# One constants load, x laid out by partition, and the input normalisation split into three groups

## The reference, cut to what matters

```python
def _ln(x, w, b):
    mu = jnp.mean(x, axis=-1, keepdims=True)
    var = jnp.mean(jnp.square(x - mu), axis=-1, keepdims=True)
    return (x - mu) * jax.lax.rsqrt(var + EPS) * w + b
...
ln_out = _ln(hidden_states, ln_w, ln_b)
q = _fp8_linear_pertensor(ln_out, wq, wq_scale, q_in_scale).reshape(b, s, g, hpg, d)
q = _ln(q, qln_w, qln_b)
...
x = x + jnp.tanh(g_xattn[0]) * _L0_xattn_ref(_layernorm(x, axis=-1), ctx_2048, ...)
x = x + jnp.tanh(g_ffn[0]) * _L0_ffn_ref(_layernorm(x, axis=-1), ...)
```

## Time and profile before

| | |
|---|---|
| median of 3 runs | 439.84 us |
| the three runs | 439.84, 442.92, 439.6 us |
| the profiled execution | 438.61 us |
| its span, from first to last instruction | 436.8 us |
| busy of the span: PE, DVE, ACT, POOL | 89%, 81%, 67%, 64% |
| first projection starts | 19.53 us |

### The profile page before, as it was taken

One profiled execution on the slowest core, in us unless ns is written; L12 is line 12 of the kernel. 1 busy time (PEld: TensorE's weight loads), 2 busy tenths in 40 slices (PEclk: granted clock), 3 DMA queues, 4 the chain that ended last, 5 costly groups with the idle time before them and its releaser, 6 DMA issues.

```text
span 436.8 us, 11224 instructions
## 1 busy us (share of the span) xinstructions
PE 387.8 (89%) x3626; PEld 288.6 (66%) x3626; DVE 352.9 (81%) x804; ACT 294.6 (67%) x621; POOL 278.0 (64%) x379
## 2 busy tenths in 40 slices
PE   0577799999999999999999999999998497999970
PEld 0445567667667767676766777676687286999960
DVE  5867979999999998999999999999889762334336
ACT  2598788777877777876877787787973315666510
POOL 2068866886787687688588677765574750366650
PEclk9999999999999999999999999999989688999995
DMA  8960868999980000000000000000194213444308
GB/s 209 261 228 2 106 90 259 253 287 286 243 230 3 0 0 0 0 0 0 0 0 0 0 0 0 0 2 2 33 434 194 96 67 98 124 132 136 99 22 277
DMA packets 34621, 45.57 MB, mean 104 GB/s; under 512 B 2970, under 2 KB 32031, under 8 KB 33696
## 3 DMA queue, kind: packets, MB, share of 16 engines
q1 hardware_dynamic: 26368, 35.34, 27.4%
q0 software_dynamic: 6944, 9.46, 9.9%
q10 hardware_dynamic: 1280, 0.41, 0.5%
HBM read 28.21 MB, written 24.19 MB: 120 GB/s over the span
## 4 chain that ended last, share of the span: by engine, by line
PE 73%; DVE 11%; ACT 4%; DMA 4%; issue 3%; POOL 3%; POOLq 0%; ACTq 0%; SPq 0%; DVEq 0%
PE proj_ps L972 18%; PE proj_ps L964 8%; PE score_ps L1001 8%; PE pv_ps L1024 8%; PE headT_ps L990 6%; PE out_ps L1034 6%; PE proj_ps L1138 4%; PE headT_ps L1138 3%; PE score_ps L990 3%; PE probT_ps L1010 3%; DMA cenf<-in_cen 2%; PE score_ps L1153 1%; DVE xs L1702 1%; DVE arena L1326 1%; PE pv_ps L1153 1%
## 5 line engine op out<-in xcount | busy, mean ns | idle before, releaser
L972 PE MATMUL proj_ps<-arena 128*128 128x512 f16 x384 | 100.0, 383 | 3.0 <-DVE arena L1356 3.0
L1364 DVE BATCH_NORM_STATS2 st<-rot 128x6 f32<-128x256 f32 x192 | 72.6, 419 | 10.6 <-ACT rot L710 10.0
L572 POOL TENSOR_TENSOR rot<-rot,cw 128x512 f32<-128x512 f32 x64 | 77.9, 1238 | 2.5
L710 ACT ACTIVATE rot<-proj_ps 128x512 f32<-128x512 f32 x96 | 56.1, 585 | 7.6 <-PE proj_ps L972 6.0
L972 PEld LDWEIGHTS proj_ps<-arena 128*128 (+1 forms) x384 | 32.5, 98 | 32.3 <-issue 3.8
L642 POOL DMA_INDIRECT ybuf<-arena,bslot x31 | 30.5, 984 | 31.3 <-DVE bslot L1612 14.6
L731 ACT ACTIVATE rot<-rot,cw 128x128 f32<-128x128 f32 x128 | 40.9, 391 | 11.0 <-POOL cw L566 10.4
L578 POOL TENSOR_TENSOR reg<-reg,rinv 128x512 f32<-128x512 f32 x32 | 33.4, 1044 | 21.9 <-DVE rinv L1374 21.9
L964 PE MATMUL proj_ps<-arena 128*128 128x512 f16 x192 | 46.7, 379 | 0.6 <-POOL arena L528 0.6
L1024 PEld LDWEIGHTS pv_ps<-reg,vv 64*128 64x128 f32 x512 | 31.1, 187 | 12.9 <-issue 9.7
L990 PE MATMUL headT_ps<-idf,rot 128*128 128x128 f32 x256 | 38.5, 273 | 0.1
(11 more groups left out here) (229 smaller groups left out, 850.2 us busy)
## 6 DMA issues: line engine op xcount, KB each, us to landing
zbuf<-fill SPq DMA_DIRECT2D x1, 16576.5 KB, 65.5
arena<-in_wffn SPq DMA_DIRECT2D x4, 1536.0 KB, 13.4
arena<-zbuf SPq DMA_DIRECT2D x30, 128.5 KB, 2.2
wkv_stage<-in_wkvN SPq DMA_DIRECT2D x1, 2048.0 KB, 15.4
wp_sb<-in_wpT POOLq DMA_DIRECT2D x1, 2048.0 KB, 16.4
wp_sb<-ybuf SPq DMA_DIRECT2D x8, 256.0 KB, 4.5
xs<-in_x SPq DMA_DIRECT2D x2, 512.0 KB, 5.5
vv<-in_wqN POOLq DMA_DIRECT2D x1, 1024.0 KB, 12.5
```

The costliest lines, as they stand in the source:

```text
L572: gp.tensor_tensor(r, r, cw[:, 4 * i:4 * i + 4].unsqueeze(2).to_broadcast([P, 4, D]), ALU.mult)\
L710: act.activation(raw[c % 2][i], proj_ps[i % 2][:, :], ACT.Copy).then_inc(proj_evac, 1)
L972: mm = pe.matmul(ps, lhs, w[kind][:, ch, 512 * b:512 * b + 512], start=(k == 0), stop=(k == 3))
L1364: ins = ve.bn_stats(st[:, 4 * i + h:4 * i + h + 2, :].rearrange("p h s -> p (h s)"), raw[c % 2][i][:, h * D:(h + 2) * D].rearrange("p (h d ...
```

## The change

The constants `colv`, `idf` and `cenf` are one tensor (`consts`) with one load, and three of the routing tables another (`tables`); the names in the code are now slices of these. ACT loads the table for Tanh ahead of the wait for the constants. x is laid out by partition on the host, so that each partition's part of a load is one contiguous run; it comes in three loads, tile 0, tiles 1 to 3, tiles 4 to 7 (`XG`). Statistics, root, sharpening and normalisation are done for each group apart. Folds 0 to 3 stand on PE ahead of the first projection, the transposes of tiles 1 to 3 behind it (they were ahead of it), and tiles 4 to 7 are normalised, transposed and moved out in the midst of step 0 (`inputs_variance(2)`, `inputs_root(2)`, `inputs_scale(2)`, `input_transposes(1)`, `inputs_out(1)`). The small operations on the gates move from the start into step 0. `xn` lies in other banks of `rot`.

```diff
+XG = [(0, 1), (1, NT // 2), (NT // 2, NT)]
...
-            for half in range(2):
-                sp.dma_start(xs[:, half * NHT * H:(half + 1) * NHT * H].rearrange("p (t d) -> p t d", t=NHT),
-                             x[half * NHT * P:(half + 1) * NHT * P, :].rearrange("(t p) d -> p t d", p=P))\
-                  .then_inc(ld_x[half], 16)
+            for i, (t0, t1) in enumerate(XG):
+                sp.dma_start(xs[:, t0 * H:t1 * H], x[:, t0 * H:t1 * H]).then_inc(ld_x[i], 16)
...
-            act.dma_start(colv[:, :], cols).then_inc(ld_cols, 16)
-            act.dma_start(idf[:, :], ident).then_inc(ld_small, 16)
-            act.dma_start(cenf[:, :], cen).then_inc(ld_small, 16)
-            act.dma_start(rowv[:, :], rowc).then_inc(ld_route, 16)
-            act.dma_start(trif[:, :], tri).then_inc(ld_route, 16)
-            act.dma_start(slots[:, :], slot).then_inc(ld_route, 16)
+            act.dma_start(consts[:, :], cols).then_inc(ld_cols, 16)
+            act.preload_act_table(ACT.Tanh)
+            act.dma_start(tables[:, :], rowc).then_inc(ld_route, 16)
...
+            inputs_root(1)
+            for j in range(4):
+                fold_high(j)
...
                 if isinstance(n, int) and n == 0:
-                    inputs_out(1)
+                    inputs_out(0)
...
                 if proj:
                     evacuate(n, c, 1)
+                if isinstance(n, int) and n == 0:
+                    inputs_root(2)
...
                 if proj:
                     values_out(t, c)
+                if isinstance(n, int) and n == 0:
+                    inputs_out(1)
```

More of the change, by code:

```diff
@@ L71 @@
 NCOL = _n
+NCONST = NCOL + 2 * P
+NTABLE = NROWV + P + NT * TOPK
 BANKS = [("k", 0), ("q", 0), ("q", 1), ("v", 0),
@@ L161, in build @@
         xs = sb("xs", [P, NT * H], F32)
-        colv = sb("colv", [P, NCOL], F32)
-        rowv = sb("rowv", [P, NROWV], F32)
-        idf = sb("idf", [P, P], F32)
-        cenf = sb("cenf", [P, P], F32)
+        consts = sb("consts", [P, NCONST], F32)
+        colv, idf, cenf = consts[:, 0:NCOL], consts[:, NCOL:NCOL + P], consts[:, NCOL + P:NCONST]
+        tables = sb("tables", [P, NTABLE], F32)
+        rowv, trif = tables[:, 0:NROWV], tables[:, NROWV:NROWV + P]
+        slots = tables[:, NROWV + P:NTABLE].bitcast(U32)
         cenb = sb("cenb", [P, P], BF16)
@@ L329, in col @@
             return colv[:, a:a + 1]
-        ld_x = [sem("ld_x0"), sem("ld_x1")]
+        ld_x = [sem(f"ld_x{i}") for i in range(3)]
         ld_cols = sem("ld_cols")
-        ld_small = sem("ld_small")
         ld_ctx = sem("ld_ctx")
@@ L686, in fold_high @@
                 act.activation(dst, src, ACT.Copy, scale=scale).then_inc(fold_hi, 1)
-            for j in range(2):
-                fold_high(j)
             act.wait_ge(xT0_done, 1)
@@ L701, in inputs_out @@
                                    scale=col("lnw", c), bias=col("lnb", c)).then_inc(xT_evac, 1)
-            inputs_out(0)
-            for j in range(2, 4):
-                fold_high(j)
             def evacuate(n, c, i):
@@ L918, in fold @@
                 mm.then_inc(fold_done, 1)
-            pe.wait_ge(ld_small, 32)
-            pe.wait_ge(cen_done, 1)
-            for j in range(2):
-                fold(j)
+            pe.wait_ge(ld_cols, 16)
             pe.wait_ge(xn_done, 1)
@@ L939, in input_transposes @@
                     mm.then_inc(xT_done, 1)
-            input_transposes(0)
+            pe.wait_ge(cen_done, 1)
+            for j in range(4):
+                fold(j)
             def project(t, c, i):
@@ L1108, in step @@
                     project(t, c, 2)
+                if isinstance(n, int) and n == 0:
+                    input_transposes(1)
                 for j in next_folds(n, 2):
@@ L1118, in step @@
                     fold(j)
+                if isinstance(n, int) and n == 1:
+                    pe.wait_ge(xT_evac, 2 * HC)
                 if heads:
@@ L1122, in step @@
                     head_transposes(n - 1, before, 2)
-                if isinstance(n, int) and n == 0:
-                    pe.wait_ge(xT_evac, 2 * HC)
                 if isinstance(n, int) and n == NU - 1:
                     pe.wait_ge(ld_wp, 16)
-            for j in range(2, 4):
-                fold(j)
             def unit_up(u, z, w):
@@ L1268, in newton, with row_stats @@
                 link(ve.tensor_tensor(r, r, a, ALU.mult))
-            def row_stats(t0, t1, loads=None):
+            def row_stats(t0, t1, load):
+                ve.wait_ge(load, 16)
                 for t in range(t0, t1):
-                    if loads and t % NHT == 0:
-                        ve.wait_ge(loads[t // NHT], 16)
                     ins = ve.bn_stats(tst[:, t, :], xs[:, t * H:(t + 1) * H])
@@ L1326, in fold_low @@
                 ve.scalar_tensor_tensor(low, src, scale, high, ALU.mult, ALU.subtract).then_inc(fold_lo, 1)
-            for j in range(2):
-                fold_low(j)
             def inputs_clip(T):
@@ L1352, in _ @@
             inputs_mag(0)
+            for j in range(2):
+                fold_low(j)
             ve.wait_ge(xmag_done, 1)
@@ L1449, in step @@
                     fold_low(j)
+                if isinstance(n, int) and n == 0:
+                    inputs_variance(2)
                 if attend:
@@ L1459, in step @@
                     fold_low(j)
+                if isinstance(n, int) and n == 0:
+                    inputs_scale(2)
+                    rows_normal(*XG[2])
+                    output_gates()
                 if attend:
```

58 lines of the change are left out of this document (29 added, 29 removed).

## The result

| | before | with the change |
|---|---|---|
| median, lowest to highest, runs | 439.28 us, 437.86 to 447.04, 16 | 445.18 us, 443.13 to 446.64, 16 |
| ratio, with its 95% interval | | 1.0119 [1.0096, 1.0143] |
| the profiled execution, its span | 438.61, 436.8 us | 443.13, 441.3 us |
| first projection | 19.53 us | 16.45 us |
| root of step 0, of step 1 on ACT | 33.40, 47.05 us | 38.76, 52.43 us |

The ratio goes by the executions in the faster of two states alone and is therefore not the quotient of the medians, which are over all executions, slower ones of the kernel before (up to 447.96 us) and one of e4 at 2167.56 us included.

The account below looks back on a forecast made before the run. A chain of waits was taken to bound the start, the root of step 0 the rest: 4.0 us won, 7.9 lost in step 0, root 3.9 later; 438.61 becomes 442.5, plus 0.9 for a median gives 443.4 us (439.8 to 445.3).

Parts of the forecast that it names:

- likeliest case: Whole kernel: the root of step 0 comes 3.9 us later, the median is 443.4 us; chance 0.60.
- rival of late loads: Start: the joined load lands at 6.5 us or more, root 5.8 later, 445.3 us or more; chance 0.13.
- T, the landing of the joined constants: Start: the joined load of constants lands at 4.6 us, for the range up to 5.6.
- First projection: End of the start: it begins at T + 10.95, 15.55 us, which is 4.0 us earlier than before.
- The 0.4 that it takes off: Start, DVE's sum of 11.35 us: 0.4 off, as pieces added this way gave 9.15 for a stretch of 8.73.
- if the weights land no later: PE ahead of the first projection: folds 2 and 3 fit on this condition; a later landing costs one for one.
- The chain of tiles 4 to 7: Step 0: statistics, root, low of fold 10, sharpening (1.0 us) and tiles follow in one line, ending at 29.55 us.
- The pause and the clock: Middle of step 0: PE idles some 4.7 us, its clock falls to half, the last projection takes 1.86 us.
- rival that the clock stays up: Step 0 behind the pause: transposes, folds and projection take half, root at 35.3, 441.4 us; chance 0.17.
- From the tiles to the root: End of step 0: transposes, folds, last projection and ACT's copies bring the root from 29.55 to 37.3 us.
- Handed on in full: Behind step 0: POOL passes any shift of its root on in full, to the end of the kernel.
- Not slower, the work falls into idle time: Step 0: DVE's idle 4.3 us take all but 1.3 of 5.6 inserted, 2.7 gained, 436.8 us; chance 0.10.

Follow-up runs that it names:

- e4: The change with sharpening and normalising of tiles 4 to 7 behind the lows of folds 12 and 13, their transposes and evacuations ending step 0; 1.0018 of the kernel before.
- e7: The change with folds 2 and 3 behind the first projection on PE, so that it doesn't wait for the q weights; 1.0150 of the kernel before.
- e8: The change with one wait added: POOL's last cast of a fold waits until tiles 4 to 7 are normalised; 1.0099 of the kernel before.
- e5: The change with twenty unread matmuls on PE in the pause ahead of the transposes of tiles 4 to 7; 1.0083 of the kernel before.
- e11: e4 with the transposes behind step 1's first projection, evacuations behind its evacuation, gates behind step 0's first statistics; 437.84 us, 0.9964 of the kernel before.
- e3: The change with all work on tiles 4 to 7, statistics to evacuations, at the end of step 0 on every engine; 1.0268 of the kernel before.
- e9: The change with the work on tiles 4 to 7 spread over step 0, the tiles normalised behind the low of fold 8; 1.0014 of the kernel before.

## Why the prediction was right, and which term was too small

The direction, the mechanism and the range held: 443.4 (439.8 to 445.3) was predicted and 445.18 measured. By the prediction's own line of 1% the kernel is slower, just over it, and that had the chance 0.25; the likeliest case lay under the line since one term was too small. That the range holds is in part luck: 445.18 is 0.1 under its upper end, which was taken from the rival of late loads, and that rival fell.

- **T, the landing of the joined constants**: 4.6 predicted, 4.04 measured (3.92 to 4.80 in the runs that load them as one in the changed order). The rival of late loads fell.
- **First projection**: 15.55 predicted, 16.45 measured, 3.08 won and not 4.0. The sum on DVE was good (rounding ends 11.07 after the landing, where the prediction has 10.8). The 0.4 that it takes off was not needed: in e7, where no weights are waited for, the first projection starts 11.21 after the landing, and the pieces add up to 11.35; the 9.15 from which the 0.4 comes can't be had from the pieces listed, which give 9.09 without ACT's two copies and 9.52 with them. The step that failed is that folds 2 and 3 fit "if the weights land no later": they land 1.0 later. Of the 0.9 by which the projection is late, 0.4 is left at the end of the statistics of tiles 4 to 7; e7 takes the wait away and wins nothing, but by another order.
- **The chain of tiles 4 to 7**: statistics end 25.72 (25.35), root ends 26.20 (25.8), the low of fold 10 ends 27.56 (27.15), sharpening ends 29.67 (28.15), tiles end 31.09 (29.55). Up to the low of fold 10 all is 0.4 late, and every piece but one has the length that it was given. **The mis-sized term is the sharpening**: 1.0 was taken from the earlier trace rows, from a place where POOL does nothing; in step 0 POOL casts folds, and it took 2.2. Holding POOL back gives 1.03 at the root (e8), most of the 1.5 by which the root was predicted too early; the median is 1.3 lower, but the intervals of the two ratios overlap.
- **The pause and the clock**: 4.7 us of pause predicted, 5.81 measured; the last projection was to take 1.86 and took 1.92. The rival that the clock stays up was priced at a root 2.0 earlier (35.3 against 37.3); keeping PE busy gives 2.03 (e5). That rival fell, and its price was right. The lower level at the start is read from durations alone: the first projection takes 1.86 us before and 1.91 now, as long as at a granted clock of 0.50, while the column reads 1.00 there (19.5 to 21.5 and 16.4 to 18.4).
- **From the tiles to the root**: 7.75 predicted (29.55 to 37.3), 7.67 measured (31.09 to 38.76).
- **Handed on in full**: yes, 5.36 at the root and 5.35 to 5.38 at every root of the loop. ACT's wait for POOL in step 1 shrinks from 2.07 to 0.45 and still ends with POOL.
- **"Not slower, the work falls into idle time"**: it fell for this order, as PE and ACT have nothing to work on in the pause. e11 has the same work behind the first projection, in an order in which PE does have something to do, and ends 1.8 us before the kernel before, with up to 1.0 of it perhaps from the clock.

## What to carry to other kernels

Work that is pushed out of the start into the first step must be placed piece by piece: who waits for each piece, what stands behind it in that engine's order, and whether another engine has work for that time; here an early start that was followed by one pause of PE was paid back twice, by the pause and by the clock after it. The duration of a small DVE operation may be carried over only from a place where POOL does the same as in the new place. To know early what a reorder at the start will do to the end, compare one row behind it (here ACT's root of step 1); the medians of thirteen kernels followed it, with 0.06 to 2.62 us on top.

## What the runs showed of the hardware that I had not expected

- A DVE operation on 4 numbers per partition took 3.90 us beside a POOL instruction of 4.05, and 0.16 without one (e3, e8). Operations that read PSUM did not suffer: the lows of folds take 0.73 to 0.77 with POOL casting or not. Nor did the statistics (0.76).
- POOL's small operations were longer in some places too: the first two of the coefficients, 0.21 us elsewhere, took 0.36 and 0.25 beside DVE's tiles in e11. In e4 they took 0.21 beside the last of the tiles, so that DVE held them is not shown.
- The same pause of PE, 2.28 us, was followed by a fallen clock in one execution (e4) and not in another (e11). PE's busy time just ahead of it, 1.34 and 1.36 us in 24 to 26, was nearly the same. After 2.47 us (e9) and 5.81 (the change) it had fallen, after 1.51 behind a busy stretch (e5) it had not; in step 1 it fell after shorter pauses, of 2.12 us in the change and 1.92 in e8, so that the wide folds took 3.59 and 3.50 us for 2.05 in e5. As far as these executions show, a kernel that has such pauses has a time that its order alone does not settle.
